# A three-part transformer block on one core: expert stages of neighbouring rows in turns, masks in row strips, router halves in one product

## What is computed

```
x = x + attn_a(layernorm(x))     # linear attention by token, 16 heads of 8, two RMS norms, a GELU MLP
x = x + ffn(layernorm(x))        # 32 experts of width 64, softmax router, best 8, weights renormalised
x = x + attn_b(layernorm(x))     # softmax attention, 16 heads, causal window of 64
x = x + ffn(layernorm(x))        # the same experts again
```

```
probs = softmax(x @ gate_w.T); the best 8 of 32, divided by their sum
for each expert e: y_e = (u * silu(g)) @ down_e.T, with [g, u] = x @ gate_up_e.T
out = sum over e of weight_e * y_e        # computed densely, all 32 experts, most weights zero
```

## Time and profile before

| | us |
|---|---|
| median of 3 runs | 1105.68 (1103.85 to 1108.86) |
| the profiled execution | 1102.44 |
| its span, first to last instruction | 1100.7 |
| TensorE busy in it | 956.2 |
| mean granted TensorE clock | 0.948 |

### The profile page before, as it was taken

How to read it: one execution, slowest core, us unless ns; L and a number is a source line. 1 busy time by engine, 2 the same in 40 slices (tenths; PEclk the granted TensorE clock), 3 DMA queues, 4 the chain that set the end, 5 groups by cost and what they waited for, 6 DMA issues and landing times.

```text
span 1100.7 us, 16771 instructions
## 1 busy us (share of the span) xinstructions
PE 956.2 (87%) x5536; PEld 659.8 (60%) x5536; DVE 655.4 (60%) x1476; ACT 623.8 (57%) x1908; POOL 618.6 (56%) x540
## 2 busy tenths in 40 slices
PE   3155999798999999797999999888999999797998
PEld 1033666575666666575666666566667666575665
DVE  5784785474764777475663777476764433475422
ACT  3236656783647555785457555785456434785431
POOL 5744886451675778442565869443565565432554
PEclk9997999896999999898999999898899999898899
DMA  4004353013453545011645363110545364011652
GB/s 158 1 10 90 80 114 87 1 40 68 88 118 89 115 99 120 5 41 26 131 95 110 77 136 87 29 40 3 116 115 117 83 139 109 1 40 30 127 118 58
DMA packets 63161, 85.68 MB, mean 78 GB/s; under 512 B 3617, under 2 KB 29026, under 8 KB 62818
## 3 DMA queue, kind: packets, MB, share of 16 engines
q1 hardware_dynamic: 63074, 84.61, 33.7%
HBM read 79.32 MB, written 5.28 MB: 77 GB/s over the span
## 4 chain that ended last, share of the span: by engine, by line
PE 71%; ACT 8%; DVE 5%; issue 4%; POOL 3%; DMA 1%; DVEq 0%; SPq 0%; POOLq 0%; ACTq 0%
PE bank L1214 19%; PE bank L1189 10%; PE bank L1191 10%; PE bank L1190 10%; PE bank L1249 4%; PE bank L1234 4%; ACT probs L788 2%; PE bank L1263 2%; PE bank L1123 2%; DVE probsT L1033 1%; PE bank L1095 1%; PE bank L1227 1%; PE bank L1089 1%; PE bank L1163 1%; PE bank L1167 1%
## 5 line engine op out<-in xcount | busy, mean ns | idle before, releaser
L614 POOL TENSOR_TENSOR work<-work,spread_w 128x512 f32<-128x512 f32 x256 | 345.5, 1359 | 245.6 <-DVE work L992 185.7
L992 DVE TENSOR_TENSOR work<-work,bank 128x512 f32<-128x512 f32 x256 | 174.8, 684 | 228.0 <-PE bank L1191 122.7
L1214 PE MATMUL bank<-work,down_w 128*128 128x512 f32 x512 | 262.1, 595 | 4.7 <-POOL work L614 2.6
L768 ACT ACTIVATE work<-bank 128x512 f32<-128x512 f32 x256 | 151.5, 596 | 186.8 <-PE bank L1191 183.0
L788 ACT ACTIVATE probs<-bank,neg_max 128x96 f32<-128x96 f32 x512 | 166.5, 363 | 43.4 <-issue 23.9
L622 POOL TENSOR_TENSOR probs<-probs,prob_inv 128x768 f32<-128x768 f32 x64 | 93.9, 1469 | 146.6 <-DVE prob_inv L1027 146.6
L1189 PE MATMUL bank<-z_hi,gate_hi 128*128 128x512 f32 x256 | 176.1, 688 | 0.0
L788 ACT ACTIVATION_READ_ACCUMULATOR probs<-bank,neg_max 128x1 f32 x512 | 118.2, 231 | 0.0
L1214 PEld LDWEIGHTS bank<-work,down_w 128*128 128x128 f32 x512 | 94.9, 188 | 31.5 <-issue 7.7
L1191 PE MATMUL bank<-z_hi,gate_lo 128*128 128x512 f32 x256 | 103.3, 403 | 0.0
L1189 PE MATMUL bank<-z_hi,up_hi 128*128 128x512 f32 x256 | 102.9, 402 | 0.0
(11 more groups left out here) (146 smaller groups left out, 1522.2 us busy)
## 6 DMA issues: line engine op xcount, KB each, us to landing
spread_w<-comb_dram SPq DMA_DIRECT2D x128, 512.0 KB, 6.7
vals<-v_dram SPq DMA_DIRECT2D x16, 384.0 KB, 3.6
x_in<-x SPq DMA_DIRECT2D x8, 256.0 KB, 3.3
v_dram<-v_tok SPq DMA_DIRECT2D x8, 256.0 KB, 2.4
out<-xs SPq DMA_DIRECT2D x4, 512.0 KB, 4.9
spread_w<-wg SPq DMA_DIRECT2D x1, 1024.0 KB, 6.8
spread_w<-wu SPq DMA_DIRECT2D x1, 1024.0 KB, 8.9
comb_dram<-combT SPq DMA_DIRECT2D x16, 64.0 KB, 1.6
```

Of the source, the lines that this page charges most:

```text
L614: pool.tensor_tensor(work[:, n % WORK], work[:, n % WORK], spread_w[:, n // EACH % 2, s % EACH], ALU.mult).then_inc(hid_gated, 1)
L768: act.activation(work[:, n % WORK], bank[GATE_BANKS[pos % DEEP]], ACT.Silu).then_inc(silu_ready, 1)
L992: dve.tensor_tensor(work[:, n % WORK], work[:, n % WORK], bank[UP_BANKS[position(row, f, s) % DEEP]], ALU.mult).then_inc(gated_ready, 1)
L1214: pe.matmul(bank[Y_BANK], down_w[:, c], work[:, n % WORK], start=(c == 0), stop=(c == CH - 1)).then_inc(down_done, 1)
```

## The change

Stages of neighbouring rows alternate. The program is written in *periods*: period p has "first" (moe 0 of row p), "second" (moe 2 of row p - 1), "third" (moe 1 of row p), "fourth" (moe 3 of row p - 1), and the attention of row p. Period 0 has only first, third and attn, period 4 only second and fourth. Streams keep their lengths (32, 64, 64, 64, 32 chunks). `PLAN` is written anew for the five places, with a `SPECIAL` plan for periods 0 and 1, the last attention and the last period. What follows attention 1 or 2 is now moe 0 of the next row, whose routing was done in "fourth", ahead of the attention; these two attentions hold one step, `y_back(3)`, at hook 2. The attention of row 0 holds the routing of row 1's moe 0, the one of row 3 that of its own moe 2. An attention has one more hook (25), between the halves of the last transposes, and `y_copy` comes after four exponentials instead of two.

```diff
-    ("attn", 0): {
-        0: own(("y_back", 1)),
-        1: own(("s_stats", 1), ("s_rstd", 1)),
...
+    "attn": {
+        2: back(("y_back", 3)),
+    },
...
+def stages_of(period):
+    if period < ROWS:
+        yield "first", period, 0
+    if period:
+        yield "second", period - 1, G
+    if period < ROWS:
+        yield "third", period, 1
+    if period:
+        yield "fourth", period - 1, G + 1
+    if period < ROWS:
+        yield "attn", period, None
```

The mask product is made from 32 rows for each head group, in the group's own rows of the array, instead of 128:

```diff
-                    pe.matmul(bank[hg][:, 0:NB * KW], ident_bf[:],
-                              window[:, min(i, 1)].rearrange("p b k -> p (b k)"), start=True, stop=False,
-                              skip_group_check=True)
+                    feats = slice(QB * hg, QB * (hg + 1))
+                    pe.matmul(bank[hg][:, 0:NB * KW], same_query[feats].rearrange("p j q -> p (j q)"),
+                              window[feats, min(i, 1)].rearrange("p b k -> p (b k)"), start=True, stop=False,
+                              tile_position=(QB * hg, 0), skip_group_check=True)
...
-                const(pool.memset(ident_bf[:], 0.0))
-                const(pool.affine_select(out=ident_bf[:], in_=ident_bf[:], compare_op=ALU.not_equal, fill=1.0, base=0,
-                                         pattern=[[-1, P]], channel_multiplier=1))
+                const(pool.memset(same_query[:], 0.0))
+                for j in range(HG):
+                    const(pool.affine_select(out=same_query[:], in_=same_query[:], compare_op=ALU.not_equal, fill=1.0,
+                                             base=-QB * j, pattern=[[0, HG], [-1, QB]], channel_multiplier=1))
```

The router's high and low weights stand side by side, so that z_hi meets both in one product; the two halves are added on VectorE (`r_sum`), where ScalarE copied the logits before (`r_copy`):

```diff
-                    for a, b, first, last in ((z_hi, router_hi, True, False), (z_hi, router_lo, False, False),
-                                              (z_lo, router_hi, False, True)):
-                        mm = pe.matmul(side[:, NE * t:NE * (t + 1)], a[:, ring, cols], b[:], start=first, stop=last)
+                    pe.matmul(side[:, 2 * NE * t:2 * NE * (t + 1)], z_hi[:, ring, cols],
+                              router_hl[:].rearrange("p a e -> p (a e)"), start=True, stop=False, skip_group_check=True)
+                    mm = pe.matmul(side[:, 2 * NE * t:2 * NE * t + NE], z_lo[:, ring, cols], router_hl[:, 0],
+                                   start=False, stop=True, skip_group_check=True)
...
+                dve.tensor_copy(logits[:], parts[:, :, 0]).then_inc(logits_ready, 1)
+                dve.wait_ge(logits_ready, 2 * fg + 1)
+                dve.tensor_tensor(logits[:], logits[:], parts[:, :, 1], ALU.add).then_inc(logits_ready, 1)
```

Rows live in two buffers that are added to in place, a row is loaded when the row two before has been through `proj`, and outputs are stored in halves:

```diff
-        x_in, x_mid, xs = (sb(n, [P, TILES, D]) for n in ("x_in", "x_mid", "xs"))
+        x_buf, xs = sb("x_buf", [P, 2, TILES, D]), sb("xs", [P, TILES, D])
...
-                wait(sp, attn_added, group(row - 1, g) + 1)
+                if row >= 2:
+                    sp.wait_ge(attn_b_done, group(row - 2, g) + 1)
...
+            def store_half(row, g):
+                sp.wait_ge(moe_done, STAGE_AT[row, G + g] + 1)
+                sp.dma_start(out_rows[row][:, T * g:T * g + T], xs[:, T * g:T * g + T]).then_inc(x_stored[g], 16)
```

707 lines of the change are left out of this document (413 added, 294 removed).

## The result

The changed kernel took 1066.1 us (median of 4 runs, 1063.9 to 1073.0) against 1104.8 us before: a ratio of 0.963, 95% interval 0.957 to 0.969. It is faster, by 3.7%, but the forecast was 1026 us with a range up to 1056. Just under half of the gain came. Where executions of one kernel lie more than 1.5% above its fastest, a ratio is taken from the others alone, while a median is that of all of them.

A forecast was written before the change was run, and what follows sets the result against it. TensorE was taken as the bound: full in expert streams, losing to waits and a lower clock in attentions. Terms -50.7, -19.9, -16.4, +7.8, +6, -5, -1.5 sum to -79.7: 1022.7 us profiled, 1026 as median, range 1006 to 1056.

The forecast's parts named there:

- the mechanism of the attentions: Attentions 1 and 2: with side work and its waits gone, about 64 us each, tiles 1 to 7 at 5.6 to 6.2.
- the -5.1: Attentions 1 and 2, start to tile 2: waits of 0.69 and 3.83 us go, transposes quicken, about 0.3 new wait.
- the 20.0 us of the sum: End of attentions 1 and 2, last pair of scores to third gate product: 20.0 us left of 29.5, so -9.5.
- the first rival: Clock falls in the quiet attentions: 22 slow tiles cost 125 us, 1150 us; at some 4 us each, 1110. Chance 4%.
- the strips as -5 us: Masks in strips, a pair side by side: 0.25 us saved in some 20 tiles, -5 us; bounds 0 and -13.
- The sum of attentions 1 to 3: Attentions 1 and 2 together -50.7 us, attention 3 -19.9; their mask savings costed separately.
- Streams: Expert streams between attentions: moved side products less cheaper routes, sum +7.8 us; additional waits +6, bounds 0 and +25.
- Attention 0: Row 0's attention keeps nearly all side work, ScalarE sets its length: 78 us against 94.4, -16.4; bounds -10 and -22.
- Attention 3: Last row's attention: start, tiles 2 and 3 save 11.9 us, its end 8; together -19.9, near 70 us.
- Routes: Streams: a route has 8 products instead of 12, 0.45 us less each, 0.9 left.
- Weights late in the streams: Rival: weights landing 9 us late at each of nine borders cost 81 us, ending at 1107. Chance 3%.
- The waits stay under other names: Rival: next in line fills half of what the waits leave; attentions gain 50 us instead of 87, 1063. Chance 10%.

The follow-up runs named there:

- The mended table: Changed kernel with full masks and edited slot table, weighT one slot behind cnorm, attention 0's y_back and second norm statistics one place earlier: 1063.0 us, 0.958 of before.
- two tables with other distances: Changed kernel with only its slot table edited, strips kept: 1089.1 us, 0.974 of before; and the mended table with full masks: 1063.0 us, 0.958.
- the third kernel with such a table: Changed kernel with full masks, the edited slot table, and attention 0's seq_turn and keys one place later each: 1067.0 us, 0.963 of before.
- the kernel with the old router: Changed kernel with the router as before, twelve products a route and ScalarE's copy of the logits: median 1096.6 us (1072.7 to 1115.1); two quicker executions 0.968 of before.

## Why the prediction was wrong

**The sign and the mechanism of the attentions were right.** The waits for the normalisation, the norm's turn and proj are gone from attentions 1 and 2, and where the clock holds, the size is right as well: attention 2 at 64.8 us, tiles of 5.1 to 6.0 us, "about 64 us". The mended table showed the mechanism of the -5.1 from the other side, when it put the norm back ahead of the normalisation and the wait of 4.4 us came with it. The end is longer than the 20.0 us of the sum (736.35 to 760.10 us in attention 2, 23.8), with 2.8 us of waits in it, where the sum had 0.9 for copies not seen.

**The step that failed most is the way the first rival was dismissed.** It said that the clock would fall in the quiet attentions; I gave it 4% "by tile 4", which ran at 1.00 without side work. But tile 4 of the kernel before has masks of full height, and the change takes exactly those away. I costed the strips as -5 us, with bounds of 0 and -13, as products that only take less of TensorE's time, and gave no bound on the other side. At full clock they do gain (0.33 us for two against 0.49, and 0.23 us a tile, as costed). What they cost beside is the clock: replacing them with full masks takes attentions 1 to 3 from 219.1 to 203.7 us, 15.4 of the 27.7 missed there, and the span of the profiled execution from 1071.3 to 1055.1 us. Strips alone in the kernel before make it 1.5% slower. The rival was not right as I wrote it either: it let all 22 tiles fall, by 5.7 or by some 4 us each, where four fell, by about 4.2. The argument that the low clock follows the long wait was weak as well: in the kernel before, the records have it fall at 945.95 us, 0.4 us into the wait of 3.83 us that ends at 949.38. The answer lay between the two, and "a quiet attention over 70 us, clock under 0.9" was the right alarm: attention 1 shows 71.9 us and 0.83.

With full masks the same transposes fill the tile as before and the clock is 0.99 in attention 2, so the transposes alone don't bring it down; no run varies them. The rule of the Trainium skill, "TensorE: Matmul & The Clock Gate", Part 4, that a transpose does not count as busy TensorE in the same way, is therefore neither shown nor refuted here. What the Trainium skill says on the same page, in "Why this matters for your kernels", that a single product of 32 rows takes the time of one of 128 and that the gain lies in several at once, agrees with the trace: one strip takes 0.33 us, one mask of full height 0.34 (at 943.54 us in the kernel before), two strips together 0.33.

**The strips are not all of the miss.** With full masks the medians are 1062.7 and 1060.2 us, still above the range. Of the 50.3 us of span, 15.4 go with the strips in attentions 1 to 3, 12.3 are left there, 15.6 are in the streams, 6.3 in attention 0, 0.8 in the tail.

**The sum of attentions 1 to 3, without the strips: 12.3 us short.** 3.8 of it is the gain that the sum gave to the strips there. 5.1 lies in attention 1, 0.9 in attention 2, 2.5 in attention 3. The sum took 25.0 us off attention 1 as if its end were that of the last one, 29.5 us from the last scores; it was 26.5 us before (500.20 to 526.67), so less could go. Of this the text names 2.1 us and takes off 0.7: 51.4 less 2.1 is 49.3, not 50.7, and "about 64 us" for both attentions would be 48.3.

**Streams: a term of the right sign, too small by 15.6 us.** Of it 8.9 is waits: 14.9 us more than before in four streams (8.0, 5.1, 1.3 and 0.5), where I took 6 with bounds of 0 and 25. The rest is mostly products: TensorE's busy time rose by 6.4 us (from 159.9) and 5.0 us in the two full streams, where I had 3.55 each, with side products priced by the last stream, in which nothing waits. Some 1 us of the 6.4 is low clock at the stream's start: with full masks it is 5.3. That the waits come from producers one slot too close was my theory, and it fell: two tables with other distances removed waits aimed at, and the sum stayed at 11.5 and 11.7 us (12.5 in the third kernel with such a table) in the first full stream, where it was 11.6, and fell from 10.7 to 9.5 in the second, which got no shorter. What sets that sum is not settled. Both tables leave the number of products of the side bank in the stream unchanged, and no run changed that number alone.

**Attention 0: -11.3 instead of -17.6.** TensorE waits for 7.4 us there, where I had counted 2.6; the difference of 4.8 is most of the 6.3 missed. The clock isn't what sets the length: with full masks the time at the low level is halved (31 to 16 us), and the attention takes 83.3 us as before, with 9.9 us of waits. No run shows what does. A part is arithmetic: the terms listed for this attention add up to 77.1 us, not to 78, which would have put the forecast 0.9 us lower still.

**Attention 3.** With full masks it takes 72.1 us, close to the "near 70". The 10.4 us above it in the changed kernel go with the strips: its clock is 0.77, with full masks 0.94.

**Routes** came near the forecast (0.6 to 0.7 us each against 0.45). **Weights late in the streams**: GpSimd, which reads the spread weights, waited for one for 0.2 us in the stream before attention 1 and not at all in the two behind it; the one long wait (15.0 us, ended at 995.3, at the end of attention 3) cost TensorE nothing. So that rival is out. **The waits stay under other names**, at 1063 us and 10%, is the case whose time came nearest, and in the streams its name describes what happened, but it was written for the attentions, and they did not lose their gain that way: the nearness of its time is luck.

The version to keep is the change with masks of full height: 0.953 and 0.957 in two sets of runs, where the change itself gave 0.963 and 0.970. Each was compared with the kernel before on its chip, not with one another.

## What to carry to other kernels

An observation that a piece of work ran at full clock speaks only for that piece of work: if the change also alters what the piece is made of, the observation is gone. When TensorE is full but not ahead (a tile of 5.5 us of its work in 5.6), a fall of its clock costs most of the factor of two (5.6 us become 9.79), and nothing in the list of waits shows it; read the granted clock of each stage and compare stages that run the same instructions. An edit that saves 0.2 us a tile in 20 tiles has a bound on the loss side too, as long as no row shows its kind of instruction in such a stretch.

## What the runs showed of the hardware

With mask products on 32 of 128 rows, two at a time, instead of products of full height, TensorE was granted its lower clock for longer, also in stretches in which it was busy without a gap (67 us against 18 in attentions 1 to 3; 132 against 65 in the kernel before). Given twice, they did so too in the profiled execution (115 us); with products of 128 rows added beside them (the fillers), or with every second pair at full height, less (36 and 30 us). That height is what matters is the reading that fits all of these, but it is argued: no run varied height alone over several values, and the wait for yT changed along with the masks.

The clock in such a stretch has two ways to go on. In one execution of the kernel with the old router the same 722 products took 65 us and 86. A tile at the low clock takes 9.79 us without a gap, and four in a row did so, with a fifth of 9.58. Where it falls is the same in the two profiles of the changed kernel, and moves when only the streams are edited; the other executions of such a kernel can differ by 42 us. So with such a kernel one profile of a stage is not a measurement of it.
